# Householder tridiagonalisation in one kernel: row products of three blocks all on VectorE, and each step's small instructions in a new order

## What is computed

```python
deg = jnp.sum(A, axis=0) + jnp.sum(A, axis=1) - jnp.diagonal(A)
d_inv_sqrt = jnp.where(deg > 0, jax.lax.rsqrt(deg), 0.0)
L_norm = d_inv_sqrt[:, None] * (jnp.diag(deg) - A) * d_inv_sqrt[None, :]
_, U = jnp.linalg.eigh(L_norm)
agg = jnp.einsum('mn,bnd->bmd', U.T, features)
...
x = x + _L0_gnn_ref(h, adj, ...)   # spectral layer, with U
x = x + _L1_gnn_ref(h, adj, ...)   # two graph convolutions, LSTM over windows
x = x + _L2_gnn_ref(h, adj, ...)   # graph convolution, batch norms
x = x + _L3_gnn_ref(h, adj, ...)   # causal attention
```

## Time and profile before

| | us |
|---|---|
| median of 3 runs | 5796.45 (5794.7 to 5798.84) |
| the profiled execution, own time | 5797.87 |
| its span in the profile | 5796.2 |
| VectorE, busy share of the span | 74% |
| TensorE, busy share (granted clock 0.655 on average) | 66% |
| first x (L297 at 47.26) to last L404 (2522.53) | 2475 |

### The profile page before, as it was taken

The page is one execution under the profiler, slowest core; times in us unless marked ns, Lnnn a source line. Parts: engine busy times, 40 slices in busy tenths (PEclk is TensorE's granted clock), DMA queues, the critical chain, the costliest instruction groups (busy, mean ns, idle before and its releaser), DMA issues. The chain is left out here.

```text
span 5796.2 us, 63099 instructions
## 1 busy us (share of the span) xinstructions
PE 3847.7 (66%) x12287; PEld 2559.1 (44%) x12287; DVE 4287.2 (74%) x24282; ACT 1342.6 (23%) x5439; POOL 51.2 (1%) x82
## 2 busy tenths in 40 slices
PE   5889998898777777754445444441056687885757
PEld 5777777777655566641112111220033343322334
DVE  7999988888888877789999999999923312223354
ACT  1222222222322333310000000000002225333444
POOL 0000000000000000000000000000000000000000
PEclk6555555555555555567677677665568898997979
DMA  0000000000000000000000000000010000000000
GB/s 8 1 1 1 1 1 1 1 1 1 1 1 1 1 1 1 1 1 0 0 1 0 0 0 0 0 1 0 0 38 12 0 0 0 0 0 0 0 9 20
DMA packets 14148, 16.01 MB, mean 3 GB/s; under 512 B 571, under 2 KB 10214, under 8 KB 13798
## 3 DMA queue, kind: packets, MB, share of 16 engines
q1 hardware_dynamic: 13798, 12.48, 0.8%
HBM read 8.28 MB, written 4.19 MB: 2 GB/s over the span
## 5 line engine op out<-in xcount | busy, mean ns | idle before, releaser
L552 DVE RECIPROCAL sturm_recip<-sturm_pivots 128x32 f32<-128x32 f32 x2560 | 713.8, 320 | 0.0
L550 DVE SCALAR_TENSOR_TENSOR sturm_pivots<-sturm_recip,neg_e,ps 128x32 f32<-128x32 f32 x2560 | 470.3, 203 | 29.3 <-PE ps L502 29.3
L277 ACT ACTIVATE vectors<-V,refl 128x4 f32<-128x4 f32 (+3 forms) x511 | 152.6, 299 | 1218.0 <-DVE refl L394 1218.0
L510 PE MATMUL ps<-sturm_flags,ident_flags 128*128 128x512 bf16 x160 | 82.7, 621 | 522.8 <-ACT sturm_flags L525 522.8
L219 PE MATMUL ps<-dot_part,ones 128*128 128x1 f32 x766 | 224.3, 362 | 271.8 <-DVE dot_part L389 271.4
L219 PEld LDWEIGHTS ps<-dot_part,ones 128*128 128x128 f32 x766 | 191.6, 311 | 428.9 <-DVE dot_part L389 428.9
L208 PE MATMUL ps<-ident,vectors 128*128 128x128 f32 x1148 | 341.9, 435 | 33.3 <-DVE vectors L404 4.7
L1236 PE MATMUL ps<-h_features,WihT 128*128 x504 | 296.0, 747 | 49.3 <-ACT gates_skip L1267 28.3
L525 ACT ACTIVATE sturm_flags<-sturm_pivots,pivot 128x1024 bf16<-128x1024 f32 x80 | 91.8, 1148 | 1007.1 <-DVE pivots_mark L555 953.1
L501 PE MATMUL ps<-points,ident 128*128 128x512 f32 x320 | 250.8, 879 | 63.5 <-DVE points_mark L536 63.5
L510 PEld LDWEIGHTS ps<-sturm_flags,ident_flags 128*128 128x128 bf16 x160 | 10.5, 110 | 589.2 <-ACT sturm_flags L525 589.2
(11 more groups left out here) (461 smaller groups left out, 9356.9 us busy)
## 6 DMA issues: line engine op xcount, KB each, us to landing
out_dram<-x SPq DMA_DIRECT2D x16, 256.0 KB, 2.3
adj<-in_adj_dram SPq DMA_DIRECT2D x1, 1024.0 KB, 5.3
l2w_in<-in_L_gnn_W_dram SPq DMA_DIRECT2D x2, 128.0 KB
Wqkv<-in_L_gnn_Wqkv_dram SPq DMA_DIRECT2D x1, 192.0 KB
L_gnn_W<-in_L_gnn_W_dram SPq DMA_DIRECT2D x2, 64.0 KB
L_gnn_Wg<-in_L_gnn_Wg_dram SPq DMA_DIRECT2D x2, 64.0 KB
x<-in_x_dram SPq DMA_DIRECT2D x4, 0.5 KB
L_gnn_Wo<-in_L_gnn_Wo_dram SPq DMA_DIRECT2D x1, 64.0 KB
```

The source lines that it names most:

```text
L550: r.inc(nc.vector.scalar_tensor_tensor(out=S,in0=R,scalar=neg_e2[:,row+dr:row+dr+1],in1=XD[h%2][dr][:,slot],op0=ALU.mult,op1=ALU.add))
L552: r.inc(nc.vector.reciprocal(R,S))
```

## The change

It does the following, all inside `tridiagonalise`:

1. Row products. `pe_tiles` gives TensorE no share in blocks 0 to 2. VectorE does all of A x there: in block 0 four products over all remaining columns instead of three and a short one, in block 1 three instead of two and a short one. The addition L378 goes.
2. Kappa. V's dots with y and with c are both made on VectorE and summed in one matmul with two columns, so kappa is one instruction; the matmul L221 goes. p becomes a column of `vectors` and is made in the next step, after x, in blocks 0 to 2 (`close`).
3. Norm. In blocks 0 and 1 one matmul sums the norm parts and all pair parts (33 columns), behind the rows' matmul; in block 2 the norm's own matmul stands first and doesn't wait for w.
4. Reflector. In blocks 1 to 3 V is made from a signed unit column and T2 (in block 3 ScalarE makes the signed column); A1 and one denominator are gone, the shift S moves behind.
5. Block 3. The rows' matmul for step m + 1 is issued at the end of step m, and VectorE completes the last entry of it in PSUM. VectorE instead of ScalarE makes u.
6. Updates. The lag is 5, 4, 4, 3; in blocks 2 and 3 the updates start with the second step of a panel, one tile a step.
7. Every wait for two or more semaphores is written in another order, and the list of each block is written out.

```diff
-def panel_lag(p): return (5,4,2,2)[panel_block(p)]
+def panel_lag(p): return (5,4,4,3)[panel_block(p)]
+def update_from(p): return (1,1,2,2)[panel_block(p)]
...
+def update_tile(m):
+
+    p=m//PANEL-1
+    if p<0: return None
+    t=panel_block(p)+m%PANEL-update_from(p)
+    return (p,t) if m%PANEL>=update_from(p) and t<NT else None
...
+def pe_tiles(m):
+
+    b=m//P
+    if b==NT-1: return range(NT-1,NT)
+    return range(0)
...
-        on_pe={0:range(1,NT),1:range(2,NT),2:range(0),3:range(3,NT)}
...
-                        pe.wait_ge(nrm_ready,m); pairs_known()
-                        nc.tensor.matmul(NORM[:,0:1],ones[:],nrm[:],start=True,stop=True).then_inc(s2_ps,1)
-                        nc.tensor.matmul(ROWS[:,X_:hi],at,XG[:,b,X_:hi],start=True,stop=True).then_inc(sel_ps,1)
-                        if L:
+                        if m>=SEP:
+                            pe.wait_ge(nrm_ready,m); pe.wait_ge(kap_ready,m-1)
+                            nc.tensor.matmul(NG[:,0:1],ones[:],gp[:,0:1],start=True,stop=True).then_inc(s2_ps,1)
+                        if m>1: pe.wait_ge(ub_ready,m-1); pe.wait_ge(w_ready,m-1)
+                        nc.tensor.matmul(ROWS[:,X_:last_slot(m)],pivot(m),XG[:,b,X_:last_slot(m)],start=True,stop=True).then_inc(sel_ps,1)
+                        if m<SEP:
+                            pe.wait_ge(nrm_ready,m)
+                            if m>1: pe.wait_ge(kap_ready,m-1); pe.wait_ge(gp_ready,m-1)
+                            nc.tensor.matmul(NG,ones[:],gp[:],start=True,stop=True).then_inc(s2_ps,1)
+                        else:
                             pe.wait_ge(gp_ready,m-1)
...
+                            nc.tensor.matmul(pair_dots(m),ones[:],halves(gp),start=True,stop=True).then_inc(g_ps,1)
                         product()
-                        for p,t in between: updated(p,t)
+                        if update_tile(m): updated(*update_tile(m))
                         pe.wait_ge(dp_ready,m)
-                        nc.tensor.matmul(DOT[:,0:1],ones[:],dp[:],start=True,stop=True).then_inc(dot_ps,1)
-                        pe.wait_ge(c_ready,m)
-                        nc.tensor.matmul(AT,at,XG[:,b,Y_:Y_+2],start=True,stop=True).then_inc(at_ps,1)
+                        nc.tensor.matmul(dots(m),ones[:],dp[:],start=True,stop=True).then_inc(dot_ps,1)
...
+                    if TAIL<=m+1<N:
+                        pe.wait_ge(ub_ready,m); pe.wait_ge(pc_ready,m)
+                        nc.tensor.matmul(ROWS[:,PC_:last_slot(m+1)],pivot(m+1),XG[:,NT-1,PC_:last_slot(m+1)],start=True,stop=True).then_inc(sel_ps,1)
...
+                    if new_rows and m<SEP: rows_copied(m//PANEL-1)
                     act.wait_ge(s2_ps,m)
...
+                    if not wide:
+                        act.wait_ge(h_ready,m-TAIL+1)
+                        nc.scalar.activation(hs[:,sl],sub[:,sl,i],ACT.Copy,scale=s[:,u,H:H+1]).then_inc(hs_ready,1)
+                    if new_rows and m>=SEP: rows_copied(m//PANEL-1)
+                    if update_tile(m): tile_copied(*update_tile(m))
...
+                def close(q):
+
+                    w=q%2; sl=slice(q//P,NT); early=TAIL<=q+1<N
+                    col=lambda j: s[:,w,j:j+1]
+                    v.wait_ge(dot_ps,q)
+                    nc.vector.scalar_tensor_tensor(out=col(KAP),in0=col(S_),scalar=dots(q)[:,1:2],in1=dots(q)[:,0:1],op0=ALU.mult,op1=ALU.add).then_inc(kap_ready,1)
+                    if q<TAIL: p_col(q)
+                    v.wait_ge(ubh_ready,q)
+                    if q>=PANEL and q%PANEL==0: v.wait_ge(gt_ps,q//PANEL)
+                    v.wait_ge(pc_ready,q)
...
+                    v.wait_ge(kap_ready,q)
+                    nc.vector.scalar_tensor_tensor(out=XG[:,sl,G_+SPREAD+slot(q)],in0=ubh[:,sl],scalar=col(KAP),in1=XG[:,sl,PC_],op0=ALU.mult,op1=ALU.add).then_inc(w_ready,1)
+                    if early:
+                        v.wait_ge(ds,half_at)
+                        k.inc(nc.vector.scalar_tensor_tensor(out=ROWS[:,G_+SPREAD+slot(q):G_+SPREAD+slot(q)+1],in0=col(KAPH),scalar=ROWS[:,G_+slot(q):G_+slot(q)+1],in1=ROWS[:,PC_:PC_+1],op0=ALU.mult,op1=ALU.add)); row_at[0]=k.at()
...
+                    def reflector():
+                        if b==0:
+                            after("S")
+                            mark("V",nc.vector.scalar_tensor_tensor(out=V[:,sl,i],in0=sub[:,sl,i],scalar=col(S_),in1=x,op0=ALU.mult,op1=ALU.add))
+                        else:
+                            if wide: after("T2","hs")
+                            else: v.wait_ge(hs_ready,m-TAIL+1); after("T2")
+                            mark("V",nc.vector.scalar_tensor_tensor(out=V[:,sl,i],in0=hs[:,sl],scalar=col(T2),in1=x,op0=ALU.mult,op1=ALU.add))
...
+                        mark("N2",nc.vector.scalar_tensor_tensor(out=col(N2_),in0=col(S_),scalar=ALPHA,in1=col(S_),op0=ALU.add,op1=ALU.mult))
...
+                        if b==0:
+                            multiply(2); inverse(); sign(); multiply(1); twice_norm(); multiply(2)
+                            by_dots(); by_rows(); shift(); add_product(); corrections(); reflector()
+                            matrix_times_x(); column_of_A()
+                        elif b==1:
+                            multiply(3); sign(); inverse(); signed_sub(); by_dots(); twice_norm(); by_rows()
+                            add_product(); corrections(); reflector()
+                            matrix_times_x(); column_of_A(); shift()
+                        else:
+                            multiply(2); inverse(); sign(); twice_norm(); signed_sub(); by_rows(); by_dots()
+                            reflector(); corrections(); shift()
+                            matrix_times_x(); column_of_A()
+                        dot_parts(); denominator(); masked(); inverses(); scaled()
+                    else:
+                        v.wait_ge(ub_ready,m-1); v.wait_ge(w_ready,m-1); v.wait_ge(ds,row_at[0])
+                        by_rows(); inverse()
+                        nc.vector.tensor_scalar(col(H),ALPHA,0.0,0.5,ALU.is_ge,ALU.subtract).then_inc(h_ready,1)
+                        by_dots(); twice_norm(); corrections()
...
+                        reflector(); column_of_A(); matrix_times_x()
+                        denominator(); masked(); inverses(); p_col(m)
+                        v.wait_ge(u_ready,m); after("V")
+                        nc.vector.tensor_scalar(XG[:,sl,G_+slot(m)],V[:,sl,i],col(T0),None,ALU.mult).then_inc(ub_ready,1)
+                        scaled()
```

More of the change, by code:

```diff
@@ new lines, in inverse, with sign, signed_sub @@
+                    def inverse():
+                        v.wait_ge(root,m)
+                        mark("R",nc.vector.reciprocal(col(R),col(Y)))
+                    def sign():
+                        v.wait_ge(sel_ps,m)
+                        mark("H",nc.vector.tensor_scalar(col(H),ALPHA,0.0,0.5,ALU.is_ge,ALU.subtract))
+                    def signed_sub():
+                        after("H")
+                        mark("hs",nc.vector.tensor_scalar(hs[:,sl],sub[:,sl,i],col(H),None,ALU.mult))
@@ new lines, in twice_norm, with shift, by_dots @@
+                    def twice_norm():
+                        after("R")
+                        mark("T2",nc.vector.scalar_tensor_tensor(out=col(T2),in0=col(R),scalar=S2,in1=col(Y),op0=ALU.mult,op1=ALU.add))
+                    def shift():
+                        after("T2","H")
+                        mark("S",nc.vector.tensor_tensor(col(S_),col(T2),col(H),ALU.mult))
+                    def by_dots():
+                        if not L: return
+                        if m<SEP: v.wait_ge(root,m)
+                        else: v.wait_ge(g_ps,m-SEP+1)
+                        mark("cy",nc.vector.tensor_tensor(cprod[:,0,sl,0:2*n].rearrange("p t (e s) -> p t e s",e=2),pairs(),pair_dots(m)[:,::-1,L[0]:L[1]].unsqueeze(1).broadcast_to([P,NB,2,n]),ALU.mult))
@@ L372, in less, with add_product @@
+                    def add_product():
+                        if tiles and wide and tiles[0]*P>m:
+                            v.wait_ge(Ax_ps,products(m))
+                            after("Ax")
+                            mark("Ax",nc.vector.tensor_tensor(px[:,NT-1:NT],px[:,NT-1:NT],ax(m),ALU.add))
                     def less(out, in0, t, q):
@@ L400, in step, with column_of_A, matrix_times_x @@
-                    if wide: v.wait_ge(c_ready,m)
-                    k.inc(nc.vector.scalar_tensor_tensor(out=pc[:,sl],in0=cc,scalar=col(S_),in1=y,op0=ALU.mult,op1=ALU.add))
-                    v.wait_ge(dot_ps,m); v.wait_ge(ds,yq_at)
+                    def column_of_A():
+                        if L: after("cor")
+                        less(cc,a[:,sl,m],sl,1).then_inc(c_ready,1)
+                    def matrix_times_x():
+                        if wide: after(*(("Ax","cor") if L else ("Ax",)))
+                        else: v.wait_ge(Ax_ps,products(m)); after("cor")
```

(1 more changed line is left out.)

236 lines of the change are left out of this document (92 added, 144 removed).

## The result

The changed kernel takes 5760.48 us (median of 4 runs, 5759.74 to 5760.82) against 5795.57 for the kernel before in the same session: a ratio of 0.9939, 95% interval 0.9926 to 0.9951. It is faster by 35 us (0.6%), where 161 were forecast; the range ended at 5690.

What follows compares the result with a forecast made beforehand. VectorE's own chain was taken to bound the first three blocks, with TensorE's round trip in the last. Blocks 2, 1, 0, 3 gain 76 + 35 + 9 + 42 = 162 us: 5635 from 5796.45, range 5595 to 5690 (8 in 10).

Steps and rivals of the forecast that it cites:

- The scaling L416: Scaling of x by two columns of scalars, without a row: 0.07 us to the next start, between 0.07 and 0.13.
- The sign product: Block 1: the sign product adds 0.07 us a step.
- a second wait: A second semaphore wait on an instruction costs 0 to 0.06 us; some four per step changed.
- The addition: Block 1, V to y: without the addition of TensorE's share from PSUM, 0.21 us a step goes.
- The head: Block 2, x to pair products: kappa 0.13, p 0.13, w 0.31, pair products 0.31; 0.88 us against 1.00 before.
- the pair sums, in PSUM at 1.44: Block 3: pair sums in PSUM at x + 1.44 give the second product at 1.47 and y at 2.10.
- Update steps: Steps updating a tile of A: block 1's excess falls from 0.62 to some 0.25 (18 us); block 0 gains 23 us.
- The root in block 0: Root moves from x + 1.91 to about x + 2.52; the reciprocal waits some 0.1 us at the block's end.
- rival 3: Blocks 0 and 1: the root becomes the bound and the kernel is 68 us slower, 5865; chance 0.02.
- rival 2: Waits between VectorE's instructions are free, only their number and columns count: 5793, no change; chance 0.03.
- Rival 1: Second waits cost full price: blocks 2 and 3 give 60 instead of 118, block 1 half; 5696, chance 0.12.
- rival 4: Larger gain, 5596: update steps like typical ones (20 us), block 0's root wait gone (10), block 3 (10); chance 0.12.

Runs made afterwards that it cites:

- the kernel with both edits: The changed kernel with the late waits written first and three tensor_scalar instructions rewritten without columns of scalars: 5627.0 us (ratio 0.9705).

## Why the prediction was wrong

The step that failed is the pricing of VectorE's small instructions: 0.07 for the scaling and for the sign product, and 0 to 0.06 for a second wait. The order of the steps came as laid out; its prices did not. The addition's price was also booked to the wrong part.

- **The clock, the rest of the run**: right. The clock is 0.50 in every stretch, and the rest moved by 0.5 us.
- **The bound**: right for blocks 0 to 2, where VectorE's own chain sets the step. In block 3 TensorE's pair sums are in the chain: L368 starts 0.04 after the matmul L234 ends.
- **The scaling L416, taken at 0.07, between 0.07 and 0.13**: the largest single error. Its spacing is 0.20 in blocks 0 to 2 and 0.18 in block 3, so some 64 us over 509 steps. In block 2 everything else from y to the next x came as laid out: 1.33 in the step shown, which is 1.20 plus this 0.13. My two ends were the nearest rows and no bounds; the price could have been put together from the trace of before, where a tensor_tensor of one column takes 0.15 and a scalar_tensor_tensor, with one column of scalars, 0.21: 0.06 to 0.07 a column, so 0.15 + 2 x 0.07 = 0.29.
- **The sign product at 0.07**: 0.14 in block 1 and 0.13 in block 2 (16 us), for the same reason.
- **The head, 0.88 to the pair products**: means of 0.98 in block 1 and 0.96 in block 2, 0.94 in the step shown. I had given both second waits 0.31; w to the pair products is 0.36. A second wait that ends late costs 0.05 to 0.10, above my "0 to 0.06". In block 0 the same shows at the first multiply, which is at x + 1.55 where I had 1.50.
- **Block 3, "the pair sums, in PSUM at 1.44"**: they are there at 1.53, since w and the pair matmul are both late by such waits. The second product is at 1.57 instead of 1.47 and y at 2.29 instead of 2.10; with the waits turned y is at 2.10. From y to x it is 1.08 instead of 0.91 + 0.08, by the columns of scalars in bu and the scaling. Together that is the 0.28 by which the step of 3.37 misses 3.09.
- **The agreement of the kernel with both edits** (each stretch within some 10 us of its forecast) is in part an offset. Its two hand-overs in the head cost 0.25 each, 0.11 less than my two 0.31, while its scaling still costs 0.14 against my 0.07.
- **The addition, "0.21 goes"**: the mechanism was wrong. It was booked to the move of the row products, and it belongs to the addition's new place; in the old place it was 0.13, and the 0.46 of the earlier trace rows is one step above the block's mean of 0.41. This hardly changed the sum, since both come in one change, but it hid that the move is a loss: 36.5 us in block 0 and 20.3 in block 1.
- **Update steps**: right. In block 0 three steps of a panel took about 0.5 more than typical ones and now about 0.2; in block 1 two took 0.6 more and now 0.1 (means over the panels, from the starts of x).
- **The root in block 0** (rival 3): VectorE's reciprocal never waited for it. The root ends at x + 2.49 on average, near the 2.52 laid out; the 0.1 of waiting that I had put at the end of the block did not come.
- **Waits free** (rival 2, and the rule of the Trainium skill, VectorE: DVE Perf Modes, "The DRAIN you can't avoid", measured there on a chain of eight tensor_copy): the trace disagrees again. Kappa to p, with nothing waited for, is 0.13, and p to w, waited for, 0.26 even with the late wait first; a mere turn of the waits was worth 90 us. That the total came nearer to this rival than to my forecast was not its doing.
- **Rival 1** had the right sign and half of the cause; it left the scaling at my price. Its 5696 does not follow from its parts: with 60 for blocks 2 and 3, half of block 1 and all of block 0 the gain is 87, so 5710.
- **Slips in the sums**: block 2's step is 2.72 + 1.20 = 3.92, not 3.95, which is 4 us more gain; block 3's is 0.35 shorter, not 0.36; rival 4's parts give 5594. None of them matters beside the miss.
- **The range** gave the unknown prices 0.1 us a step together. The whole miss is 125 us over 509 steps, 0.25 a step, and these prices are nearly all of it.

By part, then: minus 97 for the new order of the steps at the prices it met, plus 59 for the row products, and 133 more were to be had in the same order by cheaper forms and waits. (The first two make minus 38 against a kernel before of 5798.92; the result's minus 35 is against 5795.57.)

## What to carry to other kernels

In a chain of tiny VectorE instructions, price each by its operands: a column of scalars adds as much as the spacing of a whole tensor_tensor, and the same column as a broadcast tensor is free. Write the wait that ends last first, and look for places where a result handed over in 0.25 can be covered with an instruction that costs 0.07. Try the headline of a change apart from what came with it: here it was a loss inside a gain.
